# A gated attention and mixture kernel on one core: all plain fp32 matmuls of a cell in one section, all rounded products in the other

## The reference

```python
# attention, x: 4 batches x 512 tokens x 512; 16 heads; dk 64, dv 128, 64 slots
q, k, v, s = heads(x @ Wq), heads(x @ Wk), heads(x @ Wv), clip(heads(x @ Ws), -32, 32)
z = cumlogsumexp(s, over time); g = exp(z_prev - z); p = exp(s - z)
hk = hk * g_t + k_t p_t^T ;  ok_t = q_t hk           # per token t
pv = softmax(ok)                                      # over the 64 slots
hv = hv * g_t + p_t v_t^T ;  o_t = pv_t hv
o = o * rsqrt(mean(o^2) + eps) * g_norm_weight * silu(x @ Wg)
x = layernorm(x + o @ Wo)
# mixture: alpha = softmax(relu(x W1 + b1) W2 + b2); sum over 8 experts of alpha_k U_k (V_k x)
x = layernorm(x + sum_k alpha_k * U_k (V_k x))
```

## Time and profile before

| | before |
|---|---|
| median of 3 runs | 1344.43 us (1342.18 to 1344.87) |
| the profiled execution | 1344.9 us |
| its span, first to last instruction | 1343.2 us |
| mean granted clock of TensorE | 0.997 |
| PE busy | 1329.0 us (99%) |
| DVE busy | 820.8 us (61%) |
| ACT busy | 472.3 us (35%) |
| POOL busy | 276.5 us (21%) |
| DMA | 31.73 MB, mean 24 GB/s |

### The profile page before, as it was taken

How to read it: one execution, slowest core, us unless ns; L and a number is a source line. 1 busy time by engine, 2 the same in 40 slices (tenths; PEclk the granted TensorE clock), 3 DMA queues, 4 the chain that set the end, 5 groups by cost and what they waited for, 6 DMA issues and landing times.

```text
span 1343.2 us, 20338 instructions
## 1 busy us (share of the span) xinstructions
PE 1329.0 (99%) x8160; PEld 1140.7 (85%) x8160; DVE 820.8 (61%) x1559; ACT 472.3 (35%) x1391; POOL 276.5 (21%) x254
## 2 busy tenths in 40 slices
PE   8999999999999999999999999999999999999998
PEld 6888888888888888888888888888888888878886
DVE  5665666556666665566665566666555656756754
ACT  5333333343333433333324333333333333422221
POOL 3012311131112310231114111221122112212211
PEclk9999999999999999999999999999999999999999
DMA  6000200010000100010001000010000210000010
GB/s 204 17 1 0 56 1 16 1 35 22 16 1 24 32 17 1 18 39 17 1 0 48 9 16 1 25 32 17 1 24 24 64 32 1 2 0 32 16 47 32
DMA packets 35356, 31.73 MB, mean 24 GB/s; under 512 B 7616, under 2 KB 28096, under 8 KB 35264
## 3 DMA queue, kind: packets, MB, share of 16 engines
q1 hardware_dynamic: 35264, 30.44, 7.7%
HBM read 26.24 MB, written 4.19 MB: 23 GB/s over the span
## 4 chain that ended last, share of the span: by engine, by line
PE 96%; DVE 2%; DMA 1%; ACT 0%; issue 0%; POOL 0%; SPq 0%; POOLq 0%
PE p L879 19%; PE p L881 19%; PE p L880 19%; PE t L928 5%; PE s L953 3%; PE o L1069 3%; PE xb L1024 2%; PE o L1005 2%; PE o L1003 2%; PE p L953 2%; PE t L1069 2%; PE xb L978 2%; PE o L1002 2%; PE s L1371 2%; PE s L1372 2%; PE s L1373 2%
## 5 line engine op out<-in xcount | busy, mean ns | idle before, releaser
L879 PE MATMUL p<-wvg_hi,xt_hi 128*128 128x512 f32 x512 | 209.8, 410 | 0.0
L881 PE MATMUL p<-wvg_hi,xt_lo 128*128 128x512 f32 x512 | 200.9, 392 | 0.0
L880 PE MATMUL p<-wvg_lo,xt_hi 128*128 128x512 f32 x512 | 199.9, 390 | 0.0
L526 ACT ACTIVATE v_tok<-p 128x256 f32<-128x256 f32 x128 | 49.8, 389 | 328.8 <-PE p L881 328.8
L691 DVE SCALAR_TENSOR_TENSOR gate<-th,p 128x256 f32<-128x256 f32 x128 | 54.0, 422 | 164.2 <-ACT th L530 160.7
L879 PE MATMUL p<-xt_hi,wsqk_hi 128*128 128x512 f32 x380 | 148.4, 391 | 0.0
L880 PE MATMUL p<-xt_lo,wsqk_hi 128*128 128x512 f32 x380 | 148.2, 390 | 0.0
L881 PE MATMUL p<-xt_hi,wsqk_lo 128*128 128x512 f32 x380 | 147.8, 389 | 0.0
L475 POOL TENSOR_TENSOR orstd<-ovar,minus_half 128x8 f32<-128x8 f32 x32 | 52.5, 1640 | 447.4 <-DVE ovar L824 447.4
L466 POOL TENSOR_TENSOR v_lo<-v_tok,v_hi 128x256 fp32r<-128x256 f32 x96 | 83.6, 883 | 198.7 <-ACT v_hi L535 198.7
L881 PEld LDWEIGHTS p<-wvg_hi,xt_lo 128*128 128x128 f32 x512 | 96.1, 188 | 22.5
(11 more groups left out here) (241 smaller groups left out, 2846.5 us busy)
## 6 DMA issues: line engine op xcount, KB each, us to landing
raw<-in_L_attn_Wv SPq DMA_DIRECT2D x32, 128.0 KB, 2.4
raw<-in_L_attn_Wg SPq DMA_DIRECT2D x32, 128.0 KB, 3.0
raw<-in_L_attn_Wo SPq DMA_DIRECT2D x16, 256.0 KB, 2.8
out<-acc SPq DMA_DIRECT2D x16, 256.0 KB, 2.0
acc<-in_L_attn_hidden_states SPq DMA_DIRECT2D x3, 1024.0 KB, 8.0
raw<-in_L_attn_Ws SPq DMA_DIRECT2D x8, 256.0 KB, 2.8
raw<-in_L_attn_Wq SPq DMA_DIRECT2D x8, 256.0 KB, 2.9
raw<-in_L_attn_Wk SPq DMA_DIRECT2D x8, 256.0 KB, 3.0
```

Of the source, the lines that this page charges most:

```text
L526: nc.scalar.activation(v_tok[:, c, :], PB[bk][:, 0:VW], ACT.Copy).then_inc(v_done, 1)
L879: nc.tensor.matmul(out_, lh, rh, start=(k == 0), stop=False)
L880: nc.tensor.matmul(out_, lh, rl, start=False, stop=False)
L881: last = nc.tensor.matmul(out_, ll, rh, start=False, stop=(k == n - 1))
```

## The change

In the changed kernel a cell has one plain section and one rounded section on PE. The plain section: the transposes of `pz`, of `e_t` and of `k_t`; the weights of the values of the last cell; the scores of this one; the carried values; the three steps of the carried keys with, between them, the transposes of `rz_t`, the transposes of `y` of the cell *two* cells ago, and the values of the last cell for one head and then the other; and the slot sums. Then all rounded products: `vg0`, `vg1`, `wo0` to `wo3` (of two cells ago), the three narrow triples among `vg2` and `vg3`, and `s`, `k`, `q` of the next cell (`k` now ahead of `q`).

The other engines follow. `y` is made one cell later and its rows two cells after the cell's own work, so DVE's list has `ovar` and the eight `y` ahead of the two gates, and POOL's list has `orstd` first in a cell. The eight slot sums lie in another bank (`t`). The second to last and last cells have lists of their own (`LAST_USES`, rows named `xo`), since two cells' rows are still to be made there. And the load and split of W2 (`w2_high`, and a low part beside it) move from the last stage into the second to last cell, where W1's already stand.

```diff
-P_USES = ["vg0", "vg1", "wo0", "wo1", "wo2", "wo3", "vg2", "vg3", "s", "q", "k", "a0", "a1"]
-AHEAD = ("s", "q", "k", "a0", "a1")
+ROWS = ["wo0", "wo1", "wo2", "wo3"]
+P_USES = ["vg0", "vg1"] + ROWS + ["vg2", "vg3", "s", "k", "q", "a0", "a1"]
+LAST_USES = ["vg0", "vg1"] + ROWS + ["vg2", "xo0", "xo1", "xo2", "xo3", "vg3"]
+AHEAD = ("s", "k", "q", "a0", "a1")
...
+def rows_turn(of):
+    if of.b < CELLS - 2:
+        return of.shifted(2), "wo"
+    if of.b == CELLS - 2:
+        return of.shifted(1), "xo"
+    return of.shifted(1), "wo"
+def rows_of(turn, use):
+    if use[:2] == "xo" or turn.b == CELLS:
+        return turn.shifted(-1)
+    return turn.shifted(-2)
...
+        def power_gpsimd(pool, m):
+            pool.wait_ge(ovar_done, m.count(1, 1))
+            nc.gpsimd.tensor_tensor(orstd[:], ovar[:], minus_half[:], ALU.pow).then_inc(orstd_done, 1)
         def cell_gpsimd(pool, cell, J=None, last=False):
+            if not first(cell):
+                power_gpsimd(pool, cell.shifted(-1))
...
         def cell_scalar(act, cell, J=None, wo_J=None, last=False):
             nxt = cell.shifted(1)
+            if not first(cell):
+                weights_scalar(act, cell.shifted(-1))
...
+            if first(cell):
+                values_scalar(act, cell, 0)
+                act.wait_ge(e_tok_done, 1)
+                slots_high(act)
+                values_high(act, cell, 0)
+                values_scalar(act, cell, 1)
+                values_high(act, cell, 1)
+            act.wait_ge(rz_turned, cell.count(1, 1))
+            nc.scalar.activation(rz_tok[:].rearrange("p c n -> p (c n)"), RZ_BANK[:], ACT.Copy).then_inc(rz_tok_done, 1)
+            if cell.b >= 2:
+                y_high(act, cell.shifted(-2), 0)
+                y_high(act, cell.shifted(-2), 1)
+            if not first(cell):
+                squares_scalar(act, cell.shifted(-1))
             if J is not None:
                 for i, used in ((0, s_proj), (1, q_proj), (2, k_proj)):
                     split_high(act, J, i, (used, J * B))
-            values_scalar(act, cell, 0)
-            if first(cell):
-                act.wait_ge(e_tok_done, 1)
+            if not first(cell):
+                act.wait_ge(e_tok_done, cell.count(1, 1))
                 slots_high(act)
+                values_scalar(act, cell, 0)
                 values_high(act, cell, 0)
-            values_scalar(act, cell, 1)
-            act.wait_ge(rz_turned, cell.count(1, 1))
-            nc.scalar.activation(rz_tok[:].rearrange("p c n -> p (c n)"), RZ_BANK[:], ACT.Copy).then_inc(rz_tok_done, 1)
-            if not first(cell):
-                y_high(act, cell, 0)
-                y_high(act, cell, 1)
-            if not first(cell):
-                act.wait_ge(ok_summed, cell.count(1, 1))
-                slots_high(act)
-                values_high(act, cell, 0)
-            values_high(act, cell, 1)
             act.wait_ge(ok_less_top, cell.count(1, 1))
...
+            if not first(cell):
+                values_scalar(act, cell, 1)
+                values_high(act, cell, 1)
+            if last:
+                y_high(act, cell.shifted(-1), 0)
+                y_high(act, cell.shifted(-1), 1)
+            if cell.b == CELLS - 2:
+                for kt in range(KT):
+                    car.w1_high(act, kt)
+                car.w2_high(act)
+            values_scalar(act, cell, 2)
+            values_high(act, cell, 2)
...
+            if first(cell):
+                gate_vector(dve, cell, 0)
+                keep_keys(0)
+                keep_keys(1)
+                gate_vector(dve, cell, 1)
+                keep_keys(2)
+            else:
+                weights_kept(dve, prev, 0)
+                weights_kept(dve, prev, 1)
+                scores_kept(dve, cell, 0)
+                keep_keys(0)
+                scores_kept(dve, cell, 1)
+                if with_rows:
+                    y_low(dve, done_rows, 0)
+                keep_keys(1)
+                if with_rows:
+                    y_low(dve, done_rows, 1)
+                keep_keys(2)
+                variance_vector(dve, prev)
+                y_vector(dve, prev)
...
             if not first(cell):
-                add_rows(dve, cell, 0)
+                gate_vector(dve, cell, 0)
...
-            if not first(cell):
-                add_rows(dve, cell, 1)
+            if first(cell):
+                keep_values(0)
             else:
-                keep_values(0)
+                gate_vector(dve, cell, 1)
...
-            if not first(cell):
-                add_rows(dve, cell, 2)
+            if with_rows:
+                add_rows(dve, done_rows, 0)
+                add_rows(dve, done_rows, 1)
...
-            token_proj(pe, cell, 0)
+            if not first(cell):
+                if with_rows:
+                    pe.wait_ge(y_done, done_rows.count(2 * CH, 2 * CH))
+                turned_shares(pe, prev)
+            pe.wait_ge(e_done, cell.count(1, 1))
+            turned(E_BANK, [e[:, tokens(c)] for c in range(CH)], e_turned)
+            if first(cell):
+                pe.wait_ge(xt_lo_done, B * KT)
+            else:
+                pe.wait_ge(hv_kept, cell.count(CH - 1, 0))
+            pe.wait_ge(k_done, cell.count(1, 1))
+            turned(K_BANK, [k_t[:, tokens(c)] for c in range(CH - 1)], k_turned)
+            if first(cell):
+                token_proj(pe, cell, 0)
+            else:
+                slot_weights(pe, prev)
+                scores_ahead(pe, cell)
+                carried_values(pe, prev)
             pe.wait_ge(e_tok_done, cell.count(1, 1))
             pe.wait_ge(k_tok_done, cell.count(1, 1))
             running_keys(0)
-            token_proj(pe, cell, 1)
-            running_keys(1)
+            if first(cell):
+                token_proj(pe, cell, 1)
+                running_keys(1)
             pe.wait_ge(rz_done, cell.count(1, 1))
             turned(RZ_BANK, [rz_t[:, tokens(c)] for c in range(CH)], rz_turned)
+            if with_rows:
+                pe.wait_ge(weights_masked, prev.count(2, 2))
+                turned_y(pe, done_rows, 0)
+                turned_y(pe, done_rows, 1)
             if not first(cell):
-                turned_y(pe, cell, 0)
+                own_values(pe, prev, 0)
+                running_keys(1)
+                own_values(pe, prev, 1)
             running_keys(2)
             pe.wait_ge(scores_masked, cell.count(2, 2))
+            pe.wait_ge(rz_tok_done, cell.count(1, 1))
             for c in range(CH):
-                if c == 2 and not first(cell):
-                    pe.wait_ge(rz_tok_done, cell.count(1, 1))
-                    turned_y(pe, cell, 1)
-                o = OB[:, c * P:(c + 1) * P]
...
             mm.then_inc(ok_summed, 1)
             if not first(cell):
+                token_proj(pe, cell, 0)
+                token_proj(pe, cell, 1)
+            if with_rows:
                 for c in range(CH):
-                    output_rows(pe, cell, c)
+                    output_rows(pe, done_rows, c)
...
             if not last:
                 feature_proj(pe, nxt, 0, s_proj)
+                feature_proj(pe, nxt, 2, k_proj)
                 feature_proj(pe, nxt, 1, q_proj)
-                feature_proj(pe, nxt, 2, k_proj)
-            else:
-                pe.wait_ge(car.prep_lo, KT)
-            pe.wait_ge(pz_t_done, cell.count(1, 1))
-            pe.wait_ge(k_tok_done, cell.count(1, 1))
-            head_blocks(SB, e, pz_t, weights)
-            pe.wait_ge(hv_kept, cell.count(CH - 1, CH - 1))
...
+                return
...
-                if g == 0:
-                    act.wait_ge(w2_in, 16)
-                    nc.scalar.activation(w2_pad[:, :, 0:K_EXP], w2_raw[:], ACT.Copy).then_inc(w2_hi_done, 1)
-                if g == 0:
-                    dve.wait_ge(w2_hi_done, 1)
-                    nc.vector.tensor_tensor(w2_pad[:, :, K_EXP:2 * K_EXP], w2_raw[:], w2_pad[:, :, 0:K_EXP].bitcast(F32),
-                                            ALU.subtract).then_inc(w2_lo_done, 1)
                 dve.wait_ge(logits, g + 1)
```

300 lines of the change are left out of this document (161 added, 139 removed).

## The result

The changed kernel takes 1353.63 us (median of 4 runs, 1353.46 to 1353.88), the kernel before 1344.59 on the same chip. The ratio is 1.007, with a 95% interval of 1.0054 to 1.0086. It is slower, by 9.0 us; the forecast was 1350.6 (+6.2) with a range of 1343.0 to 1364.0.

What follows compares the result with a forecast made beforehand. PE, 99% busy and never waiting within a cell, was taken as the bound. 29 x (-0.11 + 0.06 + 0.27) = +6.4, +3.9, -5.2 and +1.1 gave +6.2: median 1350.6 us, range 1343.0 to 1364.0.

Steps and rivals of the forecast that it cites:

- Part 1: PE in each cell: one plain stretch instead of four saves changes of matmul kind, -0.11 us a cell.
- Part 2: Plain section: scores wait for q_t, which ACT copies last, +0.06 us a cell; the late pz_t copy is covered.
- Part 3: At wo1: PE waits for the second gate, a chain of 9.66 us against PE's 9.38, +0.27 a cell.
- Part 4: Seven weight cells: POOL's e_tok_lo keeps DVE's subtraction out, +0.56 us in each, +3.9 in all.
- Part 5: Last stage: the logits' wait for W2 and the half clock behind it go, -5.2 us.
- Part 6: First two and last two cells: extra turns and rows of two cells at once, +1.1 us.
- A: POOL's second v_lo starts before DVE's pz, so wo2 waits 0.44 us, x 30 = +13.2, 1363.8; chance 0.17.
- B: Less contention: the subtraction takes 0.69, the gate's wait is 0.09, 1345.4 us, no change; chance 0.13.
- C: Neither gate nor weight cell waits, the chain being 0.3 shorter; 1338.9 us, faster; chance 0.10.
- D: Last stage: W2's gain is not there, something else is late at the same place; 1355.8 us; chance 0.04.
- E: Plain section: the clock falls in a stretch of 15 or more transposes, +50 to +60, about 1400 us; chance 0.02.

Runs made afterwards that it cites:

- values_step_early: Changed kernel with the first narrow triple of the carried values moved on PE from behind wo3 to behind wo0; 1345.08 us, ratio to before 1.0009.
- splits_behind_values: Changed kernel with POOL's three weight splits moved from ahead of e_tok_lo to behind the second split of values, in seven weight cells; 1349.14 us.
- pz_later: Changed kernel with a small sum (tensor_reduce, some 0.27 us) on DVE ahead of the multiplication to pz; 1367.50 us.
- run 1367: Not a run's label: 1367 us is the time expected of pz_later, the changed kernel with a small sum ahead of pz; measured 1367.50 us.
- pz_loses_the_tie: Changed kernel with one small memset on DVE between the second gate and the multiplication to pz; 1354.39 us.
- values_step_and_splits: Changed kernel with both edits, of values_step_early and of splits_behind_values; 1342.55 us, ratio to before 0.9983.

## Why the prediction was right, and where it was off

The sign, the place and the mechanism of the loss were as forecast. By its own steps, with the span's +8.7 against +6.2:

**Part 1, changes of kind** (forecast -0.11 a cell, from 0.05 for each of three and a narrow triple): counted start to start, the rounded stretches of values_step_early are 0.14 shorter in sum than those of a cell of 36.07, and 0.08 shorter than those of a cell of 36.00, so 0.03 to 0.05 for each of three. That one and the same cell has several lengths, up to 0.07 apart, was not seen.

**Part 2, `q_t`** (forecast +0.06): the first tile of the scores is followed by the second after 0.183 where 0.105 is usual, +0.08; ACT's copy of `q_t` ends 0.07 before that first tile, so it is only just in time. `pz_t` costs nothing, as the step said. With 36.07 as the length before, parts 1 and 2 together are 36.007 - 36.067 = -0.06 against the forecast's -0.05; with 36.00, which the same order also takes, they are nothing.

**Part 3, the gate** (forecast +0.27): +0.32, the wait 0.18, the load 0.11, and 0.03 in the matmuls behind, which the forecast did not have. The chain was forecast at 9.66 from the end of the values with that load, and is 9.48 from the start of the squares, 9.63 with 0.04 ahead of them and the load behind. PE's own way to `wo1` was forecast at 9.38 and is 9.34. This is the mis-sized term: plain cells are 0.27 longer, not 0.22, 29 x 0.05 = 1.5 of the 2.5 us that the forecast lacks.

**Part 4, weight cells** (forecast +0.56 each, +3.9): +0.58 each, and shown to be the exclusion by splits_behind_values. The size came out nearly right because two readings were off together: the subtraction loses 0.84 where 0.75 was read, and 0.25 where 0.18 was counted already.

**Part 5, W2** (forecast -5.2): -4.8. Start by start the hole gives 3.42, as forecast. The stretch of half clock gives 1.66 and not 1.73, since at full clock these matmuls come at 0.234 and not 0.227. The rest is some 0.3 spread over the other matmuls of the stage, in steps under 0.03.

**Part 6, the ends** (forecast +1.1): +1.5, not taken apart further.

1.5 + 0.1 + 0.4 + 0.4 = 2.4 of the 2.5. All four lie on one side, so apart from the two readings inside part 4 the forecast's nearness does not come from errors that cancel.

**The rivals.** A did not occur, by 8 to 16 ns as listed, but the exclusion it rests on is real: in pz_later POOL was first and `pz` was held up. That run took 1367.5, where A gave 1363.8 and the expectation of the run 1367; as 0.33 of its delay is the added sum, it bears out the mechanism and not A's price, and no run lost the tie without such an addition. Its chance of 0.17 was drawn from the nearness of two starts alone, and pz_loses_the_tie shows that nearness was not the measure. B, C and D did not occur: the subtraction took 0.94, the waits arose, and W2's gain was there. E, the clock: the granted clock is 1.00 in both windows above and stays so from the start of the trace to 1348.8 us, behind PE's last matmul, though all 23 transposes of a cell now stand in one section with the other plain matmuls, 11 and then 12 in a row (E had read "15 or more"). The Trainium skill ("TensorE: Matmul & The Clock Gate", part 4) would let transposes count for less; here it made no difference. The Trainium skill's "GPSIMD Engine Reference" (section 1) on the shared interfaces is borne out by 0.69, 0.95 and 1.53 us for one and the same subtraction.

## What to carry to other kernels

When an engine is full, gathering its instructions by kind can bring no more than the price of the changes (0.03 to 0.05 us each here), and moving one chain of the others past another is worth far more, in either direction. In no run here did the gathering pay: with both of its waits mended (values_step_and_splits) the new order takes 1342.55 us, and the old order with the same W2 takes 1338.39. By the traces 2.3 of these 4 us are in 29 cells, 1.3 of them in the last of these and 1.1 in the weight cells, and 1.8 in the first cells and the passage to the last stage; a plain cell takes 36.007 in the one and 36.00 in the other. So what must be checked is, for each wait of the full engine, what now stands ahead of its releaser in that engine's queue, down to the last of the additions. A wait that is too short for the list of waits (0.18 us here) shows only from start to start, costs its uncovered weight load as well (0.11), and thirty of them were as much as the whole loss. And a change made of several parts is to be taken apart before it is judged: the small part here (W2, 5 us) was the gain, and it stands alone.

## What the runs showed of the hardware that was not expected

- DVE's instructions with two inputs from SBUF and POOL's do not share: the second waits for the first (subtraction 0.69, 0.95 or 1.53 us; `v_lo` 0.74 or 1.27). Overlapped by 0.39, the subtraction loses 0.25; by 0.98, 0.84: what is lost is the overlap less 0.14. With POOL's listed start 1 to 5 ns ahead, DVE still goes first; with 0.03 to 0.05 ahead (`e_tok_lo` and the subtraction in the weight cells) and with 0.32 ahead, POOL does. The first gate of a cell, whose second input `p` lies in PSUM, takes 0.41 beside POOL's `v_lo` and 0.42 without it, so it loses nothing.
- The same instructions of PE with no wait between them settle into cells of 36.00, 36.03 or 36.07 us and mostly stay there.
- A wait just met is not free: where the gate came in time, `wo1` still had 0.11 us of weight load uncovered, and some 0.03 more behind it.
